# A fused gated-recurrence layer on one core: tables, GpSimd work and the turning of g in the first chunks

## What is computed

```
xn  = layernorm(x)
pre = xn @ W + b                       # 256 -> 1024: i, f, o, z
i, f = 10*tanh((i_pre + input_bias)/10), -softplus(f_pre)
o, tz = sigmoid(o_pre), tanh(z)
scan over steps:
    m' = max(f + m, i);  i_s = exp(i - m');  f_s = exp(f + m - m')
    c = f_s*c + i_s*tz;  n = f_s*n + i_s;  h = o * c/(n + 1e-6)
x1  = x + h / rms(h) * scale
g   = layernorm(layernorm(x1)) * gamma + beta
y   = silu(g @ w1 + b1)                # 256 -> 1024; w1, w2 = (q - 128)*scales
out = layernorm(x1) + 0.5*(y @ w2 + b2)
```

## Time and profile before

| | |
|---|---|
| median of 3 runs | 329.21 us (328.18 to 329.60) |
| the profiled execution, in all | 329.68 us |
| its span, first to last instruction | 327.7 us |
| busy: PE, PEld | 307.9 (94%), 267.2 (82%) |
| busy: DVE, ACT, POOL | 262.1 (80%), 230.4 (70%), 142.4 (43%) |
| mean granted clock of TensorE | 0.978 |

### The profile page before, as it was taken

The page is one execution under the profiler, slowest core; times in us unless marked ns, Lnnn a source line. Parts: engine busy times, 40 slices in busy tenths (PEclk is TensorE's granted clock), DMA queues, the critical chain, the costliest instruction groups (busy, mean ns, idle before and its releaser), DMA issues.

```text
span 327.7 us, 4803 instructions
## 1 busy us (share of the span) xinstructions
PE 307.9 (94%) x1760; PEld 267.2 (82%) x1760; DVE 262.1 (80%) x459; ACT 230.4 (70%) x372; POOL 142.4 (43%) x140
## 2 busy tenths in 40 slices
PE   0999999998999979799999999999999999979995
PEld 0788788886987859788899888988899899869895
DVE  3998999999999896889949986688849897773430
ACT  3499956999599827479694978679584876741930
POOL 2161044002594179469992189325940122656000
PEclk9999995999999998979999999999999999999999
DMA  8990000000000300011000200010000000000101
GB/s 280 355 359 3 1 0 2 0 0 0 2 1 8 122 0 3 33 48 50 1 0 34 96 0 2 32 35 0 0 3 32 34 0 33 33 0 10 57 2 64
DMA packets 10935, 14.21 MB, mean 43 GB/s; under 512 B 672, under 2 KB 10144, under 8 KB 10656
## 3 DMA queue, kind: packets, MB, share of 16 engines
q1 hardware_dynamic: 10496, 13.12, 11.5%
q10 hardware_dynamic: 416, 0.79, 0.7%
HBM read 9.71 MB, written 4.19 MB: 42 GB/s over the span
## 4 chain that ended last, share of the span: by engine, by line
PE 34%; DVE 22%; issue 17%; POOL 16%; ACT 9%; DMA 1%; POOLq 0%; DVEq 0%
PE mm_ps L211 5%; PE mm_ps L210 5%; PE mm_ps L209 5%; PE z_ps L211 4%; PE z_ps L209 4%; PE z_ps L210 4%; POOL g L987 3%; DVE bn L732 3%; DVE g L719 2%; DVE rows L727 2%; POOL r L980 2%; DVE rec L698 2%; POOL rec L963 2%; POOL rows L1002 2%; POOL rrms L973 2%
## 5 line engine op out<-in xcount | busy, mean ns | idle before, releaser
L209 PE MATMUL z_ps<-w_hi,y_hi 128*128 128x256 f32 x256 | 74.0, 289 | 2.5 <-issue 1.4
L210 PE MATMUL z_ps<-w_lo,y_hi 128*128 128x256 f32 x256 | 72.6, 284 | 0.0
L211 PE MATMUL z_ps<-w_hi,y_lo 128*128 128x256 f32 x256 | 72.6, 283 | 0.0
L491 ACT ACTIVATE y<-mm_ps,b_all 128x512 f32<-128x512 f32 x60 | 41.4, 689 | 17.4 <-PE mm_ps L278 11.2
L209 PEld LDWEIGHTS z_ps<-w_hi,y_hi 128*128 128x128 f32 x256 | 48.8, 191 | 3.6 <-issue 1.8
L755 DVE TENSOR_TENSOR y_lo<-y,y_hi 128x512 fp32r<-128x512 f32 x64 | 42.9, 689 | 10.9 <-ACT y_hi L494 10.7
L210 PEld LDWEIGHTS z_ps<-w_lo,y_hi 128*128 128x128 f32 x256 | 48.9, 191 | 0.1
L211 PEld LDWEIGHTS z_ps<-w_hi,y_lo 128*128 128x128 f32 x256 | 48.6, 190 | 0.0
L209 PE MATMUL mm_ps<-gt_hi,w_hi 128*128 128x512 f32 x108 | 43.1, 399 | 0.0
L210 PE MATMUL mm_ps<-gt_lo,w_hi 128*128 128x512 f32 x108 | 42.8, 396 | 0.0
L211 PE MATMUL mm_ps<-gt_hi,w_lo 128*128 128x512 f32 x108 | 42.8, 396 | 0.0
(11 more groups left out here) (147 smaller groups left out, 695.6 us busy)
## 6 DMA issues: line engine op xcount, KB each, us to landing
out<-rows SPq DMA_DIRECT2D x16, 256.0 KB, 2.2
rows<-x SPq DMA_DIRECT2D x7, 512.0 KB, 6.5
q<-fc_q SPq DMA_DIRECT2D x2, 1024.0 KB, 12.1
s<-fc_scales SPq DMA_DIRECT2D x1, 1024.0 KB, 11.4
wg_raw<-fc_scales SPq DMA_DIRECT2D x1, 1024.0 KB, 11.0
wg_raw<-w_gates SPq DMA_DIRECT2D x1, 512.0 KB, 5.5
wg_raw<-w_gates ACTq DMA_DIRECT2D x1, 512.0 KB, 5.8
rows<-x ACTq DMA_DIRECT2D x1, 256.0 KB, 3.4
```

The costliest lines, as they stand in the source:

```text
L209: pe.matmul(dst, wh[w_at], ah[a_at], start=start, stop=False)
L210: pe.matmul(dst, wh[w_at], al[a_at], start=False, stop=False)
L211: return pe.matmul(dst, wl[w_at], ah[a_at], start=False, stop=stop)
L491: act.activation(y[:, j % YBUFS], fc1_bank(c, j), ACT.Silu, bias=b1_all[:, j:j + 1]).then_inc(silu_done, 1)
```

## The change

The lead-in is rearranged; nothing that is computed changes.

- ScalarE loads the set with exp and tanh first instead of the sigmoid one, so that tanh of the i gates and exp of chunk 0 need no load between them; the sigmoid set follows. Before chunk 3, the sigmoid set is loaded after the first two gate tiles (tanh runs in the silu set) and no longer before them.
- x of chunk 1 (VectorE before) and of chunk 2 (ScalarE before) is normalised by GpSimd.
- w1 is rounded by GpSimd in two blocks (half VectorE, half ScalarE before), w2 by GpSimd in two halves (ScalarE before, in one); w2's rest is made in two halves, ahead of `h_scaled(1)`.
- i*z of chunk 0 is made block by block, and each `denominators` scan waits for its block.
- g of chunk 0 is turned row tile by row tile, each as it is ready, so both blocks are complete at the end; before, block 0 was complete after four transposes.
- h of chunk 0 is turned after one gate tile of chunk 2, not two; o*c of chunk 0 comes before its Newton step, h(0) before x_low(2); ln1 of chunk 4 goes behind ln2 of chunk 1, and g_low(1) before numerators(2). On GpSimd ln2_root(1) comes before ln1_root(4).

```diff
@@ TensorE
+            def g_turned_by_rows(c):
+                pe.wait_ge(hs_done, at(c, 4, 4))
+                for n in range(TT):
+                    pe.wait_ge(g_done, at(c, 4, n + 1))
+                    for k in range(KD):
+                        ins = pe.transpose(t_ps[:, k, n * P:(n + 1) * P], g[:, n, k * P:(k + 1) * P], ident[:])
+                        if n == TT - 1:
+                            ins.then_inc(gt_ready, 1)
...
-            gates(2, range(0, 2))
+            gates(2, range(0, 1))
             h_turned(0)
-            gates(2, range(2, GJ))
+            gates(2, range(1, GJ))
             shifted_bias()
-            g_turned(0)
+            g_turned_by_rows(0)
@@ ScalarE
-            act.preload_act_table_set("sigmoid_and_others")
+            act.preload_act_table_set("exp_and_others")
...
             gates(0, I_TILES)
-            act.preload_act_table_set("natural_log_exp_and_others")
             exp_i(0)
             act.preload_act_table_set("sigmoid_and_others")
             gates(0, F_TILES)
             x_high(1)
-            gates(0, range(4, 7))
-            act.wait_ge(w1_scaled, 1)
-            act.activation(w1_hi[:, 1], w1_f[:, 1], ACT.Copy).then_inc(w1_rounded, 1)
-            gates(0, range(7, GJ))
-            x_normalised(2)
+            gates(0, range(4, GJ))
...
-            act.preload_act_table_set("sigmoid_and_others")
             gates(3, range(0, 1))
             square_sums(1)
-            gates(3, range(1, 4))
-            act.wait_ge(w2_scaled, 1)
-            act.activation(w2_hi[:], w2_f, ACT.Copy).then_inc(w2_rounded, 1)
-            gates(3, range(4, GJ))
+            gates(3, range(1, 2))
+            act.preload_act_table_set("sigmoid_and_others")
+            gates(3, range(2, GJ))
@@ VectorE
             ln1(1)
             ln1(2)
-            x_normalised(1)
             dve.wait_ge(q1_in, 16)
             dve.wait_ge(s1_in, 16)
             dve.scalar_tensor_tensor(out=w1_f, in0=q1[:], scalar=-ZERO_POINT, in1=s1[:],
                                      op0=ALU.add, op1=ALU.mult).then_inc(w1_scaled, 1)
-            dve.wait_ge(w1_scaled, 1)
-            dve.tensor_copy(w1_hi[:, 0], w1_f[:, 0]).then_inc(w1_rounded, 1)
...
-            ln1_sums(4)
             mean_square(1)
-            ln1_means(4)
+            for u in range(2):
+                dve.wait_ge(w2_rounded, u + 1)
+                dve.tensor_tensor(w2_lo[:, 4 * u:4 * u + 4], w2_f[:, 4 * u:4 * u + 4],
+                                  w2_hi[:, 4 * u:4 * u + 4].bitcast(F32), ALU.subtract).then_inc(w2_ready, 1)
             h_scaled(1)
-            dve.wait_ge(w2_rounded, 1)
-            dve.tensor_tensor(w2_lo[:], w2_f, w2_hi[:].bitcast(F32), ALU.subtract).then_inc(w2_ready, 1)
             residual(1)
             ln2_sums(1)
             ln2(1)
+            ln1(4)
@@ GpSimd
+            def x_normalised(c):
+                pool.wait_ge(ln1_r, at(c, 2, 2))
+                pool.wait_ge(xt_ready, at(c - 1, 2, 2))
+                for n in range(TT):
+                    pool.tensor_scalar(xn[:, n], rows[:, c % XBUFS, n], r1[:, c % 2, n:n + 1], nr1[:, c % 2, n:n + 1],
+                                       ALU.mult, ALU.add).then_inc(xn_done, 1)
+            def input_times_z_by_tiles(c):
+                r = rec[c % 2]
+                pool.wait_ge(i_ready, at(c, 1, 1))
+                for k in range(KD):
+                    pool.wait_ge(gate_done, at(c, 8, 5 + k))
+                    pool.tensor_tensor(r[:, 2, k], r[:, 2, k], r[:, 1, k], ALU.mult).then_inc(iz_ready, 1)
...
             ln1_root(0)
             ln1_root(1)
+            x_normalised(1)
             ln1_root(2)
-            input_times_z(0)
+            input_times_z_by_tiles(0)
+            x_normalised(2)
+            pool.wait_ge(w1_scaled, 1)
+            for k in range(KD):
+                pool.tensor_copy(w1_hi[:, k], w1_f[:, k]).then_inc(w1_rounded, 1)
...
             ln1_root(3)
+            pool.wait_ge(w2_scaled, 1)
+            for u in range(2):
+                pool.tensor_copy(w2_hi[:, 4 * u:4 * u + 4], w2_f[:, 4 * u:4 * u + 4]).then_inc(w2_rounded, 1)
             rms_root(1)
+            ln2_root(1)
             ln1_root(4)
-            ln2_root(1)
             base(0)
```

More of the change, by code:

```diff
@@ L288, in fc2 @@
                             pe.wait_ge(silu_done, at(0, 8, 6))
-                            pe.wait_ge(w2_ready, 1)
+                            pe.wait_ge(w2_ready, 2)
                     for k in range(KF):
@@ L524, in _ @@
             gates(1, range(4, GJ))
-            gates(2, I_TILES)
+            gates(2, range(0, 1))
             square_sums(0)
-            gates(2, range(2, GJ))
+            gates(2, range(1, GJ))
             g_normalised(0)
@@ L624, in x_normalised @@
                 dve.wait_ge(ln1_r, at(c, 2, 2))
-                if c >= 1:
-                    dve.wait_ge(xt_ready, at(c - 1, 2, 2))
                 for n in range(TT):
@@ L659, in denominators @@
                 s = c % 2
-                dve.wait_ge(iz_ready, at(c, 1, 1))
                 for k in blocks:
+                    dve.wait_ge(iz_ready, at(c, 2, k + 1))
                     dve.tensor_tensor_scan(rec[s][:, 1, k], f_gate[:, s, k], rec[s][:, 1, k], carry[:, s, 1, k:k + 1],
@@ L685, in input_times_z @@
                 dve.wait_ge(gate_done, at(c, 8, 6))
-                dve.tensor_tensor(r[:, 2], r[:, 2], r[:, 1], ALU.mult).then_inc(iz_ready, 1)
+                dve.tensor_tensor(r[:, 2], r[:, 2], r[:, 1], ALU.mult).then_inc(iz_ready, 2)
             def o_times_c(c):
@@ L798, in _ @@
             numerators(0)
+            o_times_c(0)
             newton(0)
             refined(0)
-            o_times_c(0)
+            h(0)
             x_low(2)
-            h(0)
             dve.wait_ge(w1_rounded, KD)
@@ L851, in _ @@
             divisor(2)
+            g_low(1)
             numerators(2)
-            g_low(1)
             newton(2)
@@ L962, in input_times_z @@
                 pool.wait_ge(gate_done, at(c, 8, 6))
-                pool.tensor_tensor(r[:, 2], r[:, 2], r[:, 1], ALU.mult).then_inc(iz_ready, 1)
+                pool.tensor_tensor(r[:, 2], r[:, 2], r[:, 1], ALU.mult).then_inc(iz_ready, 2)
+            def input_times_z_by_tiles(c):
[4 more added lines that the diff above has]
+                    pool.tensor_tensor(r[:, 2, k], r[:, 2, k], r[:, 1, k], ALU.mult).then_inc(iz_ready, 1)
             def o_times_c(c):
```

## The result

| | before | changed |
|---|---|---|
| median of the runs beside each other | 328.99 us (4 runs) | 335.69 us (4 runs) |
| ratio, 95% interval | | 1.0192 (1.0145 to 1.0240) |
| the profiled execution, in all | 329.68 us | 335.81 us |
| its span | 327.7 us | 333.9 us |
| mean granted clock | 0.978 | 0.974 |

A forecast was written before the change was run, and what follows sets the result against it. TensorE was taken to bound the kernel to 53 us, then VectorE's chain to about 140. 5.0 + 0.6 + 1.6 = 7.2 us on 329.68 gave 336.9, less 0.5 to the median: 336.4 us, range 330.0 to 340.5.

The forecast's parts named there:

- The bound: Whole kernel: TensorE sets the time to 53 us, then the chain VectorE, GpSimd, ScalarE to about 140 us.
- Part 1: Chunk 0 on ScalarE: one table load of 1.28 us less, worth 0 because TensorE waits for no gate tile before 53.
- Part 2: x of chunk 1 on GpSimd: w1_f and scans shut its tiles out; stall 3.3 plus clock 1.7, 5.0 us (2.1 to 6.5).
- The cover: Chunk 0: h, the w1 rounding and g hide behind the later TensorE; uncovered, w1 costs up to two copies of VectorE time.
- Part 3: g of chunk 0 turned row by row: fc1 starts later, at about 55.55; cost 0.6 us, bounds 0 to 0.9.
- Part 4: w2 on GpSimd: two copies of 1.1 us exclude VectorE at y_high and y_low, less 0.6 gained: 1.6 us (-0.6 to 4.2).
- (a): Lead-in: no collision, x of chunk 1 ready at 18.5, time 329.7 to 331.4 us; chance 0.15.
- (b): Faster: no collision at chunk 1, w2 copies slip under VectorE's statistics, 326.5 to 328 us; chance 0.17, shared with (d).
- (c): Worse: chunk 1's last tile behind both scans (stall 4.5), w2 copies at the addition's price, 340.8 us; chance 0.10.
- (d): The ScalarE relief reaches TensorE; time as in (b), 326.5 to 328 us; chance 0.17, shared with (b).
- right: Signs: x of chunk 1 turned after 20.5, w1_f before 18.1, a tile over 2 us, clock near 0.5, same shift to 53.
- wrong: Signs: chunk 1 transposes at 18.8, no VectorE wait for TensorE at 53, or the gap at 122 shrinking more than it moved.

The follow-up runs named there:

- table run: The kernel before with only the first ScalarE table set changed (exp and tanh first, one load less in chunk 0): 329.68 us, ratio 1.0037.
- my first two expectations: Changed kernel with VectorE waiting for GpSimd's chunk 1 x tiles before w1_f: 333.80 us, ratio 1.0149; with VectorE normalising x of chunk 1 instead: 333.50 us, ratio 1.0137.
- mostly back: Changed kernel with VectorE's wait before w1_f, old order around h of chunk 0, g by blocks, w2 on ScalarE in its old order: 330.56 us, ratio 1.0042.
- the run with one wait on VectorE: Changed kernel in which VectorE waits for the four GpSimd tiles of x of chunk 1 before w1_f: 333.80 us, ratio 1.0149.

## Why the prediction was right, by its own steps

- **The bound** (TensorE to 53 us, VectorE's chain to 140): held in the main. Where nothing else is changed behind it, the lateness of VectorE's bias addition is carried on to h of chunk 3 (1.22 and 1.34 us with the x tiles on GpSimd, 0.72 and 0.75 in the table run), and an edit at 128 us moved the end by more than its own size. That TensorE is never late before 53 is true of the one trace read: in the two with the same program up to there and a faster clock in the bias matmuls, it waits 0.56 and 0.54 us for ScalarE's g.
- **Part 1, forecast 0 with no room for more:** the step failed. I asked only whether TensorE waited for a gate tile, and not what else an earlier gate tile releases. Alone it costs: ratio 1.0037, by GpSimd's product between two scans. In the changed kernel it is covered by the stall; it also brought the scans to 19.20, in time to hold up GpSimd's tiles. ScalarE's copy of w1, "on the same terms", was not free to move either: on GpSimd it stretches VectorE by 1.75 us, hidden here by the stall.
- **Part 2, the collision:** right in mechanism and place. Of the three cases given, "two or three tiles left, ready at 22.0 to 23.2" came: w1_f got in right after the first tile, three were left, and the last was ready at 22.56. Stall 3.84 for 3.3. Clock: 5.47-3.84 = 1.63 for 1.7. That it came has luck in it: behind gaps of 1.92 us (x tiles alone) and 3.26 us (table run) no slow clock followed. Together 5.47 for 5.0. In this pair of traces 1.1 us of it came back in the bias matmuls, so the term is 4.37; against the two traces of the same program with the faster bias matmuls it is 4.7 and 5.1. So it is the trace of before, not the step "the whole shift passes into the second stretch", that makes the term small.
- **The cover.** "h, the w1 rounding and g of chunk 0 hide behind the later TensorE" held, but the list was not complete: x_low(2) behind h(0) was hidden there too. Without the stall it and the w1 copies together cost 1.98 us and its clock. For the w1 copies the forecast was right: without the cover "up to two copies of VectorE time" (2 x 1.44), measured 1.75. This second stall didn't show in the changed kernel's time, and it ruined my first two expectations.
- **Part 3:** 0.6 forecast, 0.64 in the traces at the slow clock.
- **Part 4:** 1.6 forecast. Copy 1.44 us, not 1.1; both landed on VectorE (+1.7), the wait of 0.5 before h_scaled(1) went: 1.3 in the changed kernel (from 5.07 to 6.3 or 6.5), 1.4 alone. So 1.6 came nearly true by errors against each other: each copy was longer than priced, but delayed VectorE by 0.85 us only, not by its whole length. The Trainium skill (GPSIMD Engine Reference, Elementwise — side-by-side cycle accounting) led to an estimate of 1.5 us a copy, and the trace agrees; the slope taken from the small b2 row was too low.
- **The sum:** 5.0+0.6+1.6 = 7.2 forecast; 4.4+0.6+1.3 = 6.3 in the trace, 6.2 in the spans, 6.7 between the medians, 6.3 by the ratio. With 4.7 to 5.1 for the first term it would be 6.6 to 7.0.
- **Rivals:** (a) and (b) needed tiles without a collision and are out; (c) came near in the stall and not in the copies; (d) is contradicted by the table run.
- **The signs:** those for "right" came (x of chunk 1 turned at 22.61 after a wait for GpSimd, w1_f at 16.93, tiles of 2.66 and 2.46 us, clock 0.50, everything to 53 us late by the same 5.47 to 5.49 us). Of those for "wrong" none did: TensorE's gap at 122 shrank by 1.5 us while it moved by 6.3.

What stays open: the w1 copies on GpSimd and i*z by blocks weren't run alone. They, the table set, the x tiles of chunk 2 and a few reorderings are what is left in the run "mostly back" (1.0042). There the w1 copies stand beside a Newton product of 2.05 us instead of 1.22 and a gap of TensorE of 0.74 us; the table alone had 1.0037. How the 1.0042 divides between them isn't shown. Nor is it shown how much of the loss at the end is clock: the executions of one kernel differ by as much as the smaller parts are worth.

## What to carry to other kernels

Before moving work to GpSimd, list what VectorE will do in that very window once it is free of the work: the instruction that moves up may be the one that shuts GpSimd out, and a consumer that had 0.67 us of slack waits 3.8. Free an engine only after asking whom its earlier results release. When one stall is taken out of a rearranged kernel, look for the reorderings that it covered before trusting a part-by-part undoing; edits that were made together (who rounds w2, where its rest stands) can only be undone together. Before a difference between two traces is given a cause, look for traces that share the program up to that point: the 1.1 us of the bias matmuls looked like an effect and were none.

## What I had not expected of the hardware

- A gap of about 2 us did not always bring the low clock. 2.00 us before 139 did in the kernel before; gaps of 1.92 us (x tiles alone on GpSimd) and 1.97 us (g of chunk 2 on ScalarE) were followed by a granted clock of 1.00, and so were longer ones, 3.26 us before 139.75 (table run) and 3.27 us before 144.07 (the run with one wait on VectorE). What decides it isn't shown by these runs.
- The moment at which the clock fell within a run of small matmuls moved from one execution to the next with the same program in front of it: the 32 bias matmuls took 4.76 us in the kernel before and 3.63 in both runs with o*c of chunk 3 on VectorE.
- GpSimd's float32 copy of 1024 numbers per lane into the rounded format takes 1.44 us (2.88 for two), against 2.39 for the two-input addition of the same length.
